# Rotary self-attention in a decoder kernel: two projections and two DMA row exchanges in place of four projections

## The reference, cut to what matters

```python
x_even, x_odd = x[..., ::2], x[..., 1::2]
rot_even = x_even * cos_half - x_odd * sin_half
rot_odd  = x_even * sin_half + x_odd * cos_half
...
q = (x @ wq + bq).reshape(B, S, 16, 8)      # 16 heads of 8
k = (x @ wk + bk).reshape(B, S, 16, 8)
v = (x @ wv + bv).reshape(B, S, 16, 8)
q, k = _apply_rope(q, cos, sin), _apply_rope(k, cos, sin)
scores = einsum('bhqd,bhkd->bhqk', q, k) / sqrt(8) + causal
out = einsum('bhqk,bhkd->bhqd', softmax(scores), v)
x = x + out.reshape(B, S, 128) @ wo + bo
```

## Time and profile before

| what | before |
|---|---|
| median of three runs | 2175.12 us |
| the profiled execution: its time, its span | 2172.97 us, 2171.2 us |
| PE busy (matmul) | 1942.1 us, 89% |
| PEld, DVE, ACT, POOL busy | 70%, 69%, 66%, 52% |
| layer 0's attention: first load issued, last matmul of the block | 48.98 us, 262.47 us |
| `terms` on VectorE: first, last of 128 | 60.1 us, 236.0 us |

### The profile page before, as it was taken

One profiled execution on the slowest core, in us unless ns is written; L12 is line 12 of the kernel. 1 busy time (PEld: TensorE's weight loads), 2 busy tenths in 40 slices (PEclk: granted clock), 3 DMA queues, 4 the chain that ended last, 5 costly groups with the idle time before them and its releaser, 6 DMA issues. The chain is left out here.

```text
span 2171.2 us, 63152 instructions
## 1 busy us (share of the span) xinstructions
PE 1942.1 (89%) x23942; PEld 1524.2 (70%) x23942; DVE 1490.1 (69%) x3891; ACT 1440.6 (66%) x4147; POOL 1137.4 (52%) x1477
## 2 busy tenths in 40 slices
PE   5899887399999999699969999966999999999898
PEld 2577565166666667466658888854888888888787
DVE  7699658476666555477746666657777777777567
ACT  4588645387777778488857777747666666666542
POOL 5676359377877788545422232207555445444420
PEclk9999969699999999899989999989999999999999
DMA  3000000300000000000010000010000000000101
GB/s 89 9 2 2 8 2 2 94 1 1 1 1 1 1 1 1 11 2 3 2 32 2 2 2 2 2 65 5 2 17 5 15 17 5 15 15 2 53 8 37
DMA packets 32730, 29.16 MB, mean 13 GB/s; under 512 B 5534, under 2 KB 30126, under 8 KB 32174
## 3 DMA queue, kind: packets, MB, share of 16 engines
q1 hardware_dynamic: 23214, 20.93, 3.2%
q10 hardware_dynamic: 9216, 4.20, 0.7%
HBM read 20.92 MB, written 4.19 MB: 12 GB/s over the span
## 5 line engine op out<-in xcount | busy, mean ns | idle before, releaser
L1023 POOL TENSOR_TENSOR ff_hl<-ff_hid,ff_hh 128x512 fp32r<-128x512 f32 x272 | 353.9, 1309 | 115.5 <-ACT ff_hh L1262 109.0
L1877 POOL TENSOR_TENSOR sm_zsum<-sm_zsum,sm_logits 128x512 f32<-128x512 f32 x120 | 154.6, 1288 | 274.5 <-ACT sm_logits L1903 272.8
L1191 DVE TENSOR_TENSOR ff_hid<-ff_p_b,ff_hid 128x512 f32<-128x512 f32 x240 | 164.1, 685 | 157.7 <-ACT ff_hid L1251 157.4
L1251 ACT ACTIVATE ff_hid<-ff_p_h,ff_b 128x512 f32<-128x512 f32 x272 | 185.6, 683 | 49.5 <-PE ff_p_h L1079 48.1
L1920 ACT ACTIVATE sm_sT<-sm_p_s 128x512 f32<-128x512 f32 x128 | 69.5, 595 | 220.5 <-PE sm_p_s L1713 220.5
L1262 ACT ACTIVATE ff_hh<-ff_hid 128x512 fp32r<-128x512 f32 x272 | 170.1, 625 | 40.1 <-DVE ff_hid L1191 38.0
L581 ACT ACTIVATE at_pr<-at_p_s,at_small 128x64 f32<-128x64 f32 x512 | 154.8, 329 | 61.9 <-DVE at_small L469 61.9
L1889 POOL TENSOR_TENSOR sm_logits<-sm_logits,sm_peak 128x512 f32<-128x512 f32 x128 | 163.0, 1295 | 12.7 <-ACT sm_comb L1938 12.1
L1727 PE MATMUL sm_p_l<-g_phi,g_xnT 128*128 128x256 f32 x512 | 142.6, 405 | 26.8 <-ACT sm_logits L1948 25.4
L548 POOL TENSOR_TENSOR at_kblk<-at_kT,at_heads 128x512 f32<-128x512 f32 x128 | 131.8, 1049 | 35.0 <-PE at_p_s L448 23.6
L1077 PE MATMUL ff_p_h<-ff_xh,ff_w1h 128*128 128x512 f32 x272 | 135.0, 496 | 12.3 <-ACT ff_hid L1251 8.5
(11 more groups left out here) (316 smaller groups left out, 5738.5 us busy)
## 6 DMA issues: line engine op xcount, KB each, us to landing
sm_w<-in_w_soft SPq DMA_DIRECT2D x8, 512.0 KB, 3.5
ff_whole<-in_L_ffn_rW SPq DMA_DIRECT2D x30, 128.0 KB, 2.5
early_xs<-in_x ACTq DMA_DIRECT2D x32, 64.0 KB, 1.9
ld_ctx<-in_ctx ACTq DMA_DIRECT2D x32, 64.0 KB, 2.0
x_kept<-early_xs SPq DMA_DIRECT2D x1, 2048.0 KB, 7.4
g_xnT<-x_kept SPq DMA_DIRECT2D x1, 2048.0 KB, 9.2
out_x<-sm_acc SPq DMA_DIRECT2D x8, 256.0 KB, 2.3
g_phi<-in_L_ffn_phi SPq DMA_DIRECT2D x8, 128.0 KB, 2.4
```

The source lines that it names most:

```text
L1023: eng.tensor_tensor(hl[:, q, :], hid[:, q, :], hh[:, q, :].bitcast(F32), ALU.subtract).then_inc(h_split, 1)
L1191: dve.tensor_tensor(h, p_b[e % 2][:, :], h, ALU.mult).then_inc(scaled, 1)
L1251: act.activation(hid[:, slot(u, c), :], p_h[c % 2][:, :], ACT.Gelu, bias=b1[:, c:c + 1]).then_inc(gelud, 1)
L1877: pool.tensor_tensor(z, z, logits[:, j % RING_L, :, :], ALU.add).then_inc(summed, 1)
```

## The change

The exchanged projections go. TensorE makes only `wq` and `wk` products. VectorE still computes four terms, all four from these two: first the two sine terms, then the two cosine terms. The sine tables now carry the sign of the partition that the value will go to. SyncE then moves the sine terms of both queries and keys between neighbouring partitions: two transfers within SBUF, even rows to odd rows and odd rows to even rows (64 partitions, stride two, 1 KB each, 64 KB a transfer) into a new tile `turned`. GpSimd waits for both transfers and adds `turned` to the cosine terms. There are two buffers of `terms` and `turned`, with one transfer semaphore for each. Two loads of weights go, and the bias columns are three instead of five.

```diff
-    names = ["wq", "wk", "wv", "wo"] + (["wqs", "wks"] if rope else [])
+    names = ["wq", "wk", "wv", "wo"]
...
+            for k in range(NT if rope else 0):
+                sync.wait_ge(rope_terms, 4 * (k + 1))
+                if has(k - 2):
+                    sync.wait_ge(q_ready, k - 1)
+                    sync.wait_ge(k_ready, k - 1)
+                for odd in range(2):
+                    sync.dma_start(turned[1 - odd:P:2, k % 2, :, :], terms[odd:P:2, k % 2, 1, :, :]).then_inc(rope_turned[k % 2], 16)
...
-                            pe.wait_ge(k_terms, 2 * k)
+                            pe.wait_ge(rope_terms, 4 * k)
...
-                    for i, n in enumerate(["wq", "wqs", "wk", "wks"] if rope else ["wq", "wk"]):
+                    for i, n in enumerate(["wq", "wk"]):
...
+                        dve.wait_ge(rope_turned[v], 32 * (k // 2))
+                    for part in (1, 0):
+                        for i in range(2):
+                            dve.scalar_tensor_tensor(
+                                terms[:, v, part, i, :].rearrange("p (b s) -> p b s", b=PER),
+                                p_qk[:, i * P:(i + 1) * P].rearrange("p (b s) -> p b s", b=PER), cols[:, i:i + 1],
+                                row_bc(table[:, 2 * i + part, :], PER), ALU.add, ALU.mult).then_inc(rope_terms, 1)
...
-                    pool.wait_ge(q_terms, 2 * (k + 1))
+                    pool.wait_ge(rope_turned[k % 2], 32 * (k // 2 + 1))
+                    pool.wait_ge(rope_terms, 4 * (k + 1))
...
-                    pool.tensor_tensor(qT[:, v, :], terms[:, v % 2, 0, :], terms[:, v % 2, 1, :], ALU.add).then_inc(q_ready, 1)
-                    pool.wait_ge(k_terms, 2 * (k + 1))
+                    pool.tensor_tensor(qT[:, v, :], terms[:, v % 2, 0, 0, :], turned[:, v % 2, 0, :], ALU.add).then_inc(q_ready, 1)
...
-                    pool.tensor_tensor(kT[:, v, :], terms[:, v % 2, 2, :], terms[:, v % 2, 3, :], ALU.add).then_inc(k_ready, 1)
+                    pool.tensor_tensor(kT[:, v, :], terms[:, v % 2, 0, 1, :], turned[:, v % 2, 1, :], ALU.add).then_inc(k_ready, 1)
...
-    c["c_rope8"] = np.concatenate([cos * scale, sin * scale, cos, sin], 1)
+    c["c_rope8"] = np.concatenate([cos * scale, -sin * scale, cos, -sin], 1)
```

More of the change, by code:

```diff
@@ L314, in attention @@
             table = m.sb("table", [P, 4, S])
-            cols = m.sb("cols", [P, 5])
+            cols = m.sb("cols", [P, 3])
             bo = m.sb("bo", [P, D])
@@ L318, in attention @@
                       (bo[:, :], io["w0_bo"].rearrange("(a d) -> a d", a=1).to_broadcast([P, D]))]
-            terms = m.sb("terms", [P, 2, 4, P])
+            terms = m.sb("terms", [P, 2, 2, 2, P])
+            turned = m.sb("turned", [P, 2, 2, P])
             bvb = m.sb("bvb", [P, P])
@@ L334, in attention @@
         qk_done, v_done, v_copied = m.sem("qk_done"), m.sem("v_done"), m.sem("v_copied")
-        q_terms, k_terms, q_ready, k_ready, kblk_ready = (m.sem(n) for n in ("q_terms", "k_terms", "q_ready", "k_ready", "kblk_ready"))
+        rope_terms, q_ready, k_ready, kblk_ready = (m.sem(n) for n in ("rope_terms", "q_ready", "k_ready", "kblk_ready"))
+        rope_turned = m.sems("rope_turned", 2)
         s_done, maxed, exped, centred, c_exped = (m.sem(n) for n in ("s_done", "maxed", "exped", "centred", "c_exped"))
@@ L458, in _ @@
             if rope:
-                dve.tensor_copy(bvb[:, :], cols[:, 4:5].to_broadcast([P, P])).then_inc(bv_spread, 1)
+                dve.tensor_copy(bvb[:, :], cols[:, 2:3].to_broadcast([P, P])).then_inc(bv_spread, 1)
                 dve.wait_ge(bv_done, 1)
@@ L2037 @@
     arrays["w_gbl"] = np.stack([a["L1_xattn_gamma_l"], a["L1_xattn_beta_l"]], 1)
-    swap = np.arange(D) ^ 1
     for n in ("wq", "wk", "wv", "wo"):
@@ L2041 @@
         arrays["w1_" + n] = a["L1_attn_W" + n[1]].T
-    arrays["w0_wqs"], arrays["w0_wks"] = a["L0_attn_wq"][:, swap], a["L0_attn_wk"][:, swap]
     bq, bk = a["L0_attn_bq"], a["L0_attn_bk"]
-    arrays["w0_cols"] = np.stack([bq, bq[swap], bk, bk[swap], a["L0_attn_bv"]], 1)
+    arrays["w0_cols"] = np.stack([bq, bk, a["L0_attn_bv"]], 1)
     arrays["w0_bo"] = a["L0_attn_bo"]
```

## The result

| | before | after |
|---|---|---|
| median, four runs each | 2173.48 us | 2193.59 us |
| ratio, 95% interval | | 1.0094 [1.0077, 1.0112] |
| block of layer 0's attention, first load to the next block's first load | 214.5 us | 232.1 us |

The kernel is 20 us slower: slower as forecast, but by three times the 6.6 us and outside the range. The block takes 17.5 us of it in the two traces. The few us that are left lie in blocks that the change doesn't touch; from the trace of before to that of after these moved by between -2.0 and +3.9 us. So I judge runs by their block too.

A forecast was written before the change was run, and what follows sets the result against it. PE bounds the loop at 5.84 us a turn, DVE close behind at 5.66. The transfer loop adds 9.0 us, the start gives back 0.95 and 1.4: +6.6, so 2181.7 us, range 2175 to 2190.

The forecast's parts named there:

- L: Time from the end of DVE's terms to the start of POOL's add that waits for the transfers; forecast 2.41 us.
- the start: Before the first scores: two fewer weight loads give -0.95 us and an earlier first key block -1.4, together -2.35.
- DVE's own turn of 5.66 us: Main loop: DVE's turn without waits, 0.32 + 4.22 + 1.12 us, close behind PE's 5.84.
- 0.45 us of PE's work is hidden but for 0.18: Main loop: two fewer matmuls save PE about 0.45 us a turn, but DVE's turn limits the win to 0.18.
- rival 1: The transfer is hidden, needing L under 1.36 us, and the kernel gets faster: -7.0 us, or 2168; chance 8%.
- The loop, two turns in L + 4.30 + 5.66: From terms through SP, transfers and POOL to L273, then a DVE turn: mean turn 6.19 us, +9.0 over 26 turns.
- DVE issues the same operations and its turn stays at 5.66: Main loop: DVE can't follow PE's saving, because its operations and its turn of 5.66 us are unchanged.
- the ramp: From the first scores to turn 2: scores come at their old pace, set by ACT and DVE; change forecast 0.
- one landing time for all tiles: The second transfer within SBUF lands in 1.9 us, taken for every turn of the loop.
- My upper 3.0: The upper value of L, in us, counted to for the range; a load's 3.1 us landing would have given 3.6.
- Rival 4: TensorE, busy 5.39 in 6.19 us, falls to the lower clock in places, some 2195 us; chance 2%.

The follow-up runs named there:

- 1/sqrt first: Changed kernel with GpSimd's 1/sqrt (L264, L266) moved first in its turn, before queries, keys and spread keys: 2171.63 us, ratio 0.9987, block 209.9.
- the same order without the exchange: Changed kernel with GpSimd's 1/sqrt first in its turn and no transfers, output not rotated rightly: 2166.38 us, ratio 0.9966, block 208.4.
- POOL's order unchanged: Changed kernel without its transfers and the wait for them, output not rotated rightly: 2171.84 us, ratio 0.9984, block 212.6.
- the reduce: Changed kernel with layer 0's copy L496 written as a max over one element: 2192.62 us, ratio 1.0088, block 230.3.
- eight traces: Traces of the changed kernel, the run with 32 spare TensorE matmuls, and the six others with transfers and without extra loads.
- one shift: Changed kernel with 32 spare small matmuls on TensorE at the block's start: 2206.77 us in its one run, block 243.8.
- imitation: Changed kernel with a 16 KB row loaded from device memory ahead of each pair of transfers: 2194.60 us, ratio 1.0085, block 230.9.

## Why the prediction was wrong in size

The forecast was +6.6 us and the measurement +20.1. In the terms of the sum the 13.5 us between them are: L too short 1.9, DVE's turn stretched in the loop 2.6, late landings and the clock after one of them 4.4, the turns ahead of the loop 1.0, the start 0.9, and 2.6 outside the block.

- **DVE's own turn of 5.66 us** was right where nothing new meets it: it is the turn of the two runs with 1/sqrt first and the copy, with and without the exchange. That 0.45 us of PE's work is hidden but for 0.18 was right as well, and rival 1's -7 us is near what the same order without the exchange gave (-7.5 by the medians, -6.1 in the block). With POOL's order unchanged that gain isn't there, which I had not seen: L273 then meets L548.
- **The loop, two turns in L + 4.30 + 5.66,** was right, with its alternation: to 0.01 us in two quiet pairs, to 0.05 in the pair shown.
- **L** was 2.53 in quiet turns, not 2.41. The landing of the second transfer was right (1.93, 1.9 taken; the first takes 1.76), but the second issue comes 0.5 to 0.6 after the first, not 0.37. By the formula (2.53 + 9.96) / 2 = 6.245 and 26 turns come to +10.9 (from the measured 5.825) instead of +9.0. The 2.15 us that the prediction quotes from the Trainium skill is, in that section, a fit for transfers issued from GpSimd, which the prediction doesn't say; issued from SyncE they landed in 1.93. And its L of 2.66 would have added 3.25 us, not below 3.
- **Failed: "DVE issues the same operations and its turn stays at 5.66".** The wait moves POOL's L550 to L567 by 2.5 us or more, on top of DVE's copy L496, which before ran between L555 and L264, while POOL stood idle. In the ramp, which I had called unchanged, three turns grew by 1.0 us in all, and the reduce takes 0.7 of it back. In the loop the stretch is some 2.6: the 26 turns lie 7.0 us above the formula with the copy and 4.4 with the reduce (there with a DVE turn of 5.72).
- **Failed: one landing time for all tiles.** The rest, some 4.4 us, is put down to late landings and the clock after the worst of them. My upper 3.0 was for all turns at once; in the changed kernel three tiles went to 3.1 to 4.2, each with an instruction packet on the pair. Rival 4's 2195 lies close to the 2194 measured, but its falling clock gives only a small part: in the 26 turns the clock was at 0.50 for 9.4 us in all (from 216.5 to 223.3 and from 257.4 us), behind the latest landing, and the turn from 213.39 took 7.38 us, 1.7 more than the quickest of the loop (5.68). Since a long L273 wait is followed by a turn without any, lateness is absorbed in one parity of turns and paid in full in the other. This split is arithmetic on single traces, good to a microsecond or two.
- **The start** gave -1.5 instead of -2.35: L ahead of the first scores was 2.59, and the first scores (L458) took 1.99 us, as in the stretch with the clock at 0.50, where before they took 1.38.

On the stretch the Trainium skill has the rule ("SBUF — State Buffer", "Who interferes with whom"): an fp32 copy or tensor_scalar within SBUF can use a port pair that it shares with GpSimd, and whichever starts second waits for the whole instruction, while a reduce never does. By this rule the trace agrees for the copy: it reached 0.88 us, and every stretched copy of the changed kernel ends 0.08 to 0.09 us after the GpSimd operation that was running when it started; the reduce stayed at 0.29. For L273 it agrees in part: its 0.62 end 0.08 us after L548, but by the records L273 had started 0.09 ahead of it. I had not weighed the rule, since before no copy was stretched.

Settled: the order of POOL's work around the wait carries the loss, and the copy's stretch is of its form. Shown by their times against the pair's in eight traces and by one shift, not by imitation: the instruction packets. Arithmetic on single traces: how the 7.0 us above the formula are split. Open: the 2 to 4 us outside the block.

## What to carry to other kernels

Before you put a transfer behind a wait on an in-order engine, list what stands behind that wait and who needs it; here moving two 0.2 to 0.55 us operations ahead of it was worth 22 us in the block. A wait also moves the engine's other work in time, so look at which operations it will meet on a shared resource. Price a transfer on a critical loop by its tail as well as its median, or give it a turn of slack.

## What the runs showed of the hardware

- A pair of 64 KB transfers within SBUF with partition stride two: each lands in 1.7 to 1.9 us when no instruction packet meets it, near the loads' 1.7 and 2.0; the issues take 0.46 and about 0.56 us on SyncE.
- Beside GpSimd's tensor_tensor a 128x128 fp32 copy on VectorE took up to 1.12 us instead of 0.23, a tensor_scalar 0.62 instead of 0.40 (0.35 where GpSimd stood idle), a reduce over one element always 0.29.
- A 64 KB transfer that met a 16 KB packet of the instruction queue landed in up to 4.0 us. A packet that had ended 0.8 us after the pair's first issue, or started 2.1 us after it, cost nothing, but for the two pairs named above.
